# First scan of a four-layer kernel, stage one: the square taken from y, the clip as a minimum inside the cube, and the low part issued later

## The reference, cut to what matters

```
def _derivative(q, p, drive, coupling, bias):
    i_couple = jnp.tanh(q) @ coupling.T
    dq = q - q ** 3 / 3.0 - p + drive + i_couple + bias
    dp = EPSILON * (q + ALPHA - BETA * p)
    return (dq, dp)
def _rk4_step(q, p, drive, coupling, bias):
    dq1, dp1 = _derivative(q, p, ...)
    dq2, dp2 = _derivative(q + 0.5 * DT * dq1, p + 0.5 * DT * dp1, ...)
    dq3, dp3 = _derivative(q + 0.5 * DT * dq2, p + 0.5 * DT * dp2, ...)
    dq4, dp4 = _derivative(q + DT * dq3, p + DT * dp3, ...)
    q_next = q + DT / 6.0 * (dq1 + 2 * dq2 + 2 * dq3 + dq4)
    p_next = p + DT / 6.0 * (dp1 + 2 * dp2 + 2 * dp3 + dp4)
    q_next = jnp.clip(q_next, -CLAMP, CLAMP)      # CLAMP = 20
```

## Time and profile before

| what | value |
|---|---|
| time, median of 3 runs | 2069.48 us (2069.31 to 2070.36) |
| time of the profiled execution | 2070.81 us |
| its span, first to last instruction | 2069.1 us |
| VectorE busy | 1418.7 us, 69% |
| TensorE matmul busy | 1437.8 us, 69% |
| GpSimd busy | 591.5 us, 29% |
| stretch from the first to the last y of the scan | about 263 to 951 us |

### The profile page before, as it was taken

How to read it: one execution, slowest core, us unless ns; L and a number is a source line. 1 busy time by engine, 2 the same in 40 slices (tenths; PEclk the granted TensorE clock), 3 DMA queues, 4 the chain that set the end, 5 groups by cost and what they waited for, 6 DMA issues and landing times. The chain is left out here.

```text
span 2069.1 us, 48431 instructions
## 1 busy us (share of the span) xinstructions
PE 1437.8 (69%) x16570; PEld 1116.0 (54%) x16570; DVE 1418.7 (69%) x6953; ACT 742.6 (36%) x2889; POOL 591.5 (29%) x1597
## 2 busy tenths in 40 slices
PE   6898844444444444445599999999957866677665
PEld 4476533333333333332488888888825754555554
DVE  4457699989989998997556555555546345555554
ACT  4568522222222222223334333433344443333322
POOL 1045355545545554553311111111124000000010
PEclk9979955555555555556799999999988975555555
DMA  3000000000000000002100000000020000000000
GB/s 108 0 1 2 1 2 2 2 3 2 2 3 2 2 2 3 2 2 87 46 1 31 16 18 15 16 1 1 1 81 31 1 0 2 2 2 13 4 11 23
DMA packets 15097, 28.20 MB, mean 14 GB/s; under 512 B 1692, under 2 KB 9464, under 8 KB 14584
## 3 DMA queue, kind: packets, MB, share of 16 engines
q1 hardware_dynamic: 14672, 24.93, 3.5%
q10 hardware_dynamic: 168, 0.04, 0.0%
HBM read 20.77 MB, written 4.19 MB: 12 GB/s over the span
## 5 line engine op out<-in xcount | busy, mean ns | idle before, releaser
L817 PE MATMUL bank<-s_tanh_hi,coup_hi 128*128 128x16 f16 x2048 | 141.6, 180 | 344.6 <-ACT s_tanh_hi L807 329.5
L817 PEld LDWEIGHTS bank<-s_tanh_hi,coup_hi 128*128 128x128 f16 x2048 | 95.0, 108 | 392.0 <-ACT s_tanh_hi L807 376.7
L807 ACT ACTIVATE s_tanh_hi<-s_s 128x32 f16<-128x32 f32 x384 | 88.0, 229 | 394.9 <-DVE s_s L679 394.9
L1245 POOL TENSOR_TENSOR prob<-prob,inv 128x512 f32<-128x512 f32 x64 | 66.5, 1040 | 426.4 <-DVE inv L1211 426.4
L1523 PE MATMUL bank<-h_hi,w_h_hi 128*128 128x16 f16 x1536 | 95.2, 176 | 111.6 <-DVE h_hi L1663 111.6
L1131 ACT ACTIVATE prob<-bank,neg_max 128x128 f32<-128x128 f32 x256 | 90.5, 366 | 215.5 <-DVE neg_max L1180 215.5
L1687 POOL TENSOR_TENSOR x<-x,h 128x32 f32<-128x32 f32 x128 | 34.4, 269 | 447.9 <-DVE h L1666 447.9
L817 PE MATMUL bank<-s_tanh_lo,coup_hi 128*128 128x16 f16 x2048 | 141.3, 180 | 22.3 <-DVE s_tanh_lo L673 9.7
L1523 PEld LDWEIGHTS bank<-h_hi,w_h_hi 128*128 128x128 f16 x1536 | 70.7, 105 | 158.0 <-DVE h_hi L1663 158.0
L817 PE MATMUL bank<-s_tanh_hi,coup_lo 128*128 128x16 f16 x2048 | 130.2, 174 | 0.0
L817 PEld LDWEIGHTS bank<-s_tanh_lo,coup_hi 128*128 128x128 f16 x2048 | 94.6, 107 | 61.9 <-DVE s_tanh_lo L673 33.8
(11 more groups left out here) (286 smaller groups left out, 4713.6 us busy)
## 6 DMA issues: line engine op xcount, KB each, us to landing
w_stage<-in_L_cond_qkv_w_dram SPq DMA_DIRECT2D x12, 512.0 KB, 5.2
x_tok<-in_x_dram SPq DMA_DIRECT2D x4, 512.0 KB, 5.8
ow_stage<-in_L_cond_out_w_dram SPq DMA_DIRECT2D x4, 512.0 KB, 5.4
x_in<-x SPq DMA_DIRECT2D x1, 2048.0 KB, 11.4
x_in_sb<-x_in SPq DMA_DIRECT2D x1, 2048.0 KB, 12.0
out_dram<-o_sb SPq DMA_DIRECT2D x64, 32.0 KB, 1.6
ada_w<-in_L_cond_ada_w_dram SPq DMA_DIRECT2D x1, 1536.0 KB, 12.2
v_bias<-in_L_cond_qkv_b_dram SPq DMA_DIRECT2D x4, 256.0 KB, 5.6
```

What stands on the lines that cost most here:

```text
L807: A.activation(th_hi[:, :], s, ACT.Tanh).then_inc(hi_ready, 1)
L817: ins = nc.tensor.matmul(coupled[:, B * m:B * m + B], w[:, o:o + P], th[:, B * c:B * c + B], start=(first and c == 0 and m == 0), stop=(la ...
L1245: G.tensor_tensor(prob[:, grp % 2, :, :], prob[:, grp % 2, :, :], inv[:, grp % 2, :].unsqueeze(2).broadcast_to([P, HG, T]), MUL).then_inc( ...
```

## The change

In stage one alone:

- The square is taken of y, not of the clipped q in `trace`. It is issued as the last operation of the step before (and once ahead of the loop), behind the clip, with no wait between.
- The clip is applied to the square instead: the cube is min(sq, 400) * q, a plain cube of the clipped q.
- The term that the -3 had carried moves into base1, which becomes q * (1 + h) + pm, with h = DT / 2. It turns from a TENSOR_TENSOR into a SCALAR_TENSOR_TENSOR.
- The low part is issued behind cube and base1; before, it stood behind square and base1 and ahead of the cube. rest stands right behind it and ahead of m1.
- The counts follow: M2_AT and M3_AT are one lower, GpSimd's first wait is for count ND * j - 1, which is still the clip. ND stays 30.

```diff
-    M2_AT, M3_AT = 9, 16
+    M2_AT, M3_AT = 8, 15
...
             STT(pm, p1, -h, drive[:, 0:W1], MUL, ADD).then_inc(init, 1)
-            dve.wait_ge(init, 6)
+            V.tensor_tensor(sq, y, y, MUL).then_inc(init, 1)
+            dve.wait_ge(init, 7)
...
                     if j:
                         after(ND * j)
-                    ns = do(V.tensor_tensor(sq, q, q, MUL))
-                    do(V.tensor_tensor(base1, pm, q, ADD))
+                    do(STT(cube, sq, CLAMP * CLAMP, q, ALU.min, MUL))
+                    nb = do(STT(base1, q, 1.0 + h, pm, MUL, ADD))
                     low(1)
-                    after(ns)
-                    nc_ = do(STT(cube, sq, -3.0, q, ADD, MUL))
+                    after(nb)
+                    nr = do(STT(rest, cube, -h / 3, base1, MUL, ADD))
                     nm = do(STT(m1, p1, -BETA, q, MUL, ADD))
-                    after(nc_)
-                    nr = do(STT(rest, cube, -h / 3, base1, MUL, ADD))
                     after(nm)
                     n = do(STT(p2, m1, h * EPSILON, p1, MUL, ADD))
                     advance(1, s2, 0, nr)
...
                     do(V.tensor_scalar(trace[:, bass.ds(lap * (LAP * W1) + W1 * (j + 1), W1)], y,
                                        CLAMP, -CLAMP, ALU.min, ALU.max))
+                    do(V.tensor_tensor(sq, y, y, MUL))
...
                     if j:
-                        pool.wait_ge(dve_done, ND * j)
+                        pool.wait_ge(dve_done, ND * j - 1)
```

## The result

The changed kernel takes 2078.32 us (median of 6, 2076.9 to 2078.94) where the kernel before takes 2069.92 in the same rounds: a ratio of 1.0043, 95% interval 1.0031 to 1.0054. It is slower by about 8.4 us. That is inside the stated range of 2066 to 2081, but outside the likeliest case's own range of 2069.5 to 2075, which had said 2.6 us; slower had a chance of 0.28.

A forecast was written before the change was run, and what follows sets the result against it. VectorE's order of operations in stage one was taken as the bound: 124 steps x 0.02 = 2.5 us plus 0.1 at the laps gave 2.6 on 2069.48, about 2072.0 us, range 2066 to 2081.

The forecast's parts named there:

- likeliest case: Stage one's order as laid out, +0.00 to +0.04 a step: about 2072.0 us, own range 2069.5 to 2075; chance 0.44.
- The bound: Scan, stage one: VectorE's order of operations sets s2's start; TensorE's side has 0.12 us of slack.
- The new forms cost nothing: Stage one's cube with the minimum and base1 as SCALAR_TENSOR_TENSOR each taken at 0.18 us, bounds 0.18 and 0.19.
- The layout of stage one: Start times from y to s2: base1 held in low's stead, m1 held, p2 waiting for m1, s2 1.55 behind y.
- +0.02 a step: Stage one: s2 at 593.47 in place of 593.45; over 124 steps 2.5 us, bounds 0 and 5.0.
- my bound of +0.04: Stage one: the most that s2 would come later per step if all roundings fell badly.
- rest loses the race: Rival, stage one: rest starts with GpSimd's qd2 and is held, +0.08 a step, 10 us, 2079 to 2080; chance 0.15.
- The laps: Between laps of the scan: the moved square and the one ahead of the loop cost 0.1 us in all.
- Stages two to four keep their lengths: Later stages shift with s2 and keep their lengths, apart from a rival where base3 wins its race, up to 3 us.
- The hold of full length: Rival, stage one: base1 starts only when GpSimd's qd1 ends, +0.13 a step, 16 us, about 2086; chance 0.03.
- the first tenth of a microsecond: Rule: a VectorE operation starting that soon within a GpSimd TENSOR_TENSOR is held; a hold costs 0.05 to 0.10.
- The number of operations: Rival: only VectorE's operation count matters, 30 as before, so 2069.5; chance 0.20, shared with all slack cancelling.

The follow-up runs named there:

- e1: Changed kernel with m1 issued ahead of rest again: 2071.09 us against 2068.78 for the kernel before, ratio 1.0010.
- e2: Changed kernel with the low part ahead of the cube again and base1 waiting for the clip alone: 2058.58 us against 2068.78 for the kernel before, ratio 0.9952.
- e7: Changed kernel with GpSimd's first wait one count later, on the square and not the clip: 2070.78 us against 2072.55 for the kernel before, ratio 0.9996.
- e3: Changed kernel with GpSimd's first wait two counts later, on base1 and not the clip: 2075.16 us against 2068.78 for the kernel before, ratio 1.0031.
- e9: Changed kernel with one operation less ahead of the scan's loop (p1 computed without the copy): ratio 1.0015 to the kernel before.
- e5: Kernel before with one idle operation more (an unread square of y) ahead of the loop: 2074.93 us against 2072.55, ratio 1.0012.
- e4: Kernel before with m1 issued behind rest in stage one, all else as before: 2095.46 us, ratio 1.0129.
- e8: Changed kernel with low part early, GpSimd's first wait on the square, one operation less ahead of the loop: 2050.37 us against 2071.78 for the kernel before.

## Why the prediction was right, point by point

**The bound.** That stage one is bound by VectorE's chain and that TensorE has 0.12 of slack was right: e1, e2 and e7 moved s2 just as these two chains say. ("Every other engine at half or less" is a little off: the earlier trace rows has GpSimd at 355 of 688, 52%.)

**The new forms cost nothing.** Right: the cube lasts 0.19, base1 0.18 where it isn't held (e3, e7).

**The layout of stage one.** Right in order and, for the common step, in each hold. The square, the cube, base1, low and rest fall within 0.03 of the stated places. The term "+0.02 a step" was too small: s2 is 0.05 later, 124 x 0.05 = 6.2 us in place of 2.5. It was the end of the chain that was mis-sized: m1 starts 0.11 behind rest and is held for 0.24, p2 comes at 1.47 and not 1.44, s2 0.11 to 0.12 behind it. So TensorE's last four stand 0.37 ahead of s2 and not 0.31 to 0.33: its side no longer comes close. Even my bound of +0.04 was short, since I added rounded rows with the small end each time. e1 shows that this chain through m1 and p2 is the cause, e7 that the hold by GpSimd is what makes it decide.

**rest loses the race.** The price was 0.08 a step beyond y + 1.53; where it occurs, it costs 0.15 beyond the common step (1.73 against 1.58), since m1 is caught by the next GpSimd operation. But it occurs in 6 of 124 steps, about 1 us, and not in every one. The time landed near this rival's 2079 by other terms, and that is no proof of it. The range reached up to 2081 for this rival's sake: that it holds the 2078.3 is largely luck, since about 6.1 us of the common step, 0.9 of lost races and 2.2 at the laps, less 1.7 in stages two and three, came together there.

**The laps.** Wrong: "0.1 in all" measured 2.2 us. The square's own place costs next to nothing there: in e9, with the square behind the clip, the heads idle 12.5 us (12.6 before) and the steps that cross laps take 30.1 (29.5 before). What costs is that one operation more stands ahead of the loop, which also moves the loop's code; e5 and e9 show it from both sides. The heads' idle time grew by 3.1 us, the steps that cross laps by only 2.2; why they differ stays open. No run moved the code alone, so that its place is the cause is argued and not shown.

**Stages two to four keep their lengths.** Nearly: stage two gave back 1.4 us, as base3 won its race more often. In e5, with the loop of the kernel before, stage two is at 1.234 as well, so it doesn't take the edit in stage one to get there. Whether it varies from one execution to the next or with what stands ahead of the loop, these single traces don't tell.

**The hold of full length.** Its price, 0.13 a step, did not come. base1 starts at 591.95, inside qd1 (591.91 to 592.16), and ends at 592.20; had its 0.18 begun only at qd1's end, it would have ended at 592.34 and low would stand at about 592.26, not 592.13. The rule of the Trainium skill in SBUF — State Buffer, section SBUF: two separate sides, an exclusive lock that goes to the one that starts first, fits as to who is held: in e7 base1, 0.05 ahead, is free and low is held; in e3, with GpSimd away, neither is. The prediction, and its rule of "the first tenth of a microsecond", missed what the rows say on how long. A held operation ends 0.04 to 0.05 behind GpSimd's end: base1 at 592.20 behind 592.16, low in the earlier trace rows at 592.97 behind 592.92, base3 in the earlier trace rows at 594.78 behind 594.74. It is so throughout: in the scans of the eleven traces 4579 TENSOR_TENSOR and SCALAR_TENSOR_TENSOR operations of VectorE that don't read PSUM last 0.23 us or more, and 4459 of them start behind a GpSimd TENSOR_TENSOR and end 0.04 to 0.06 behind its end (the other 120 start behind none; what draws them out is open). So a hold does last until GpSimd's operation ends, which agrees with the Trainium skill's "for the whole instruction", but the held operation has only its last 0.04 to 0.06 still to go. A hold costs little (0.05 to 0.10 here) for that reason, and e4's rest, which would end at that point anyway (568.17 behind 568.12), pays nothing. Which part of an operation's record needs the lock, no run here shows.

**The number of operations.** The rival falls by e4: two lines exchanged, 1.3% slower. The Trainium skill's advice in VectorE: DVE Perf Modes, Rules for kernel authors, to minimise operations and not semaphores, doesn't fit this chain of short dependent operations: an unwaited one starts 0.11 behind the last (591.84, 591.95), one that waits for it 0.22 (591.62, 591.84). As for the section on the DRAIN, which the prediction set against the rows: it adds itself that a next operation that is not held (by an earlier one of VectorE) starts earlier, and there the rows agree with it.

## What to carry to other kernels

In a chain of short operations, ask of each edit which operation is last to be ready for the bound one, and put work that others wait for (here m1, for p2) ahead of work that stands ready anyway. Where a second engine reads the same memory, its release is a knob of its own: one count in its wait was worth as much as the edit cost. Look then at where the other engine's operation ends and not only at where it starts, since that is where a held one comes free. And when a loop's restart shows in the profile, an operation added ahead of the loop is not free just because it runs once.

## What the runs showed of the hardware that was not expected

- The hold works both ways. Where VectorE's operation starts just ahead of GpSimd's TENSOR_TENSOR, or up to 0.03 us behind it and yet wins, it keeps its 0.18 to 0.19 and GpSimd's is drawn out from 0.25 to 0.28 or more; such a one ended 0.10 to 0.12 behind VectorE's in 3412 cases (qd2 in the changed kernel ends at 592.55, rest at 592.43). The next operation of VectorE then meets a later end and can be held by it, as m1 is.
- A VectorE operation that starts 0.005 to 0.03 us behind a GpSimd TENSOR_TENSOR falls on either side: 0.19 or 0.29 for the same operation in the same kernel. Held for so long it lets its successor start 0.20 later and not 0.11, and this can hand the next one to the next GpSimd operation (538.58 and 538.79 in the changed kernel).
- The restart of a lap takes VectorE 3.9 to 4.5 us with six operations ahead of the loop (before, e4, e8, e9) and 5.1 to 5.7 with seven (the change, e1 to e3, e5 to e7), whatever the order inside. What in the place of the code does this wasn't shown.
